# Two batches of a gated attention and expert kernel run as one program, with new engine orders in the batch loop

## What is computed

```python
x = x + tanh(g_xattn) * attention(layernorm(x), ctx, ctx)      # 16 heads of 16 channels
h = layernorm(x)
bids = sigmoid(h @ conf_w.T + conf_b) * wealth                 # [tokens, 8]
top_bids, selected = top_k(bids, 2)
combine = sum(one_hot(selected) * softmax(top_bids)[..., None])
x = x + tanh(g_ffn) * sum_e combine_e * expert_e(h)            # down(silu(gate h) * up h)
```

## Time and profile before

| | us |
|---|---|
| median of three runs | 1085.46 |
| lowest and highest | 1083.96, 1087.34 |
| the profiled execution | 1083.07 |
| its span, first to last instruction | 1081.4 |
| mean granted TensorE clock, share of full speed | 0.969 |

### The profile page before, as it was taken

How to read it: one execution, slowest core, us unless ns; L and a number is a source line. 1 busy time by engine, 2 the same in 40 slices (tenths; PEclk the granted TensorE clock), 3 DMA queues, 4 the chain that set the end, 5 groups by cost and what they waited for, 6 DMA issues and landing times.

```text
span 1081.4 us, 25127 instructions
## 1 busy us (share of the span) xinstructions
PE 1001.3 (93%) x8750; PEld 855.2 (79%) x8750; DVE 610.8 (56%) x1519; ACT 502.0 (46%) x796; POOL 366.3 (34%) x439
## 2 busy tenths in 40 slices
PE   5789999999999997759999999999999999999993
PEld 4556777777777765448999999999799999999993
DVE  3556777777777776455544444444554444444452
ACT  4366777777777774334323232332433323233321
POOL 1124555555555552443322212121332212122121
PEclk8799999999999999869999999999999999999997
DMA  8000111111111119258712111121262212121211
GB/s 254 27 22 22 43 45 47 41 41 41 43 51 58 41 39 371 77 182 323 256 25 40 25 35 35 25 37 23 42 229 49 37 23 40 20 40 23 37 35 17
DMA packets 48338, 77.30 MB, mean 71 GB/s; under 512 B 8616, under 2 KB 42152, under 8 KB 44456
## 3 DMA queue, kind: packets, MB, share of 16 engines
q0 software_dynamic: 18080, 50.15, 16.7%
q1 hardware_dynamic: 30216, 26.62, 8.3%
HBM read 52.09 MB, written 24.40 MB: 71 GB/s over the span
## 4 chain that ended last, share of the span: by engine, by line
PE 81%; ACT 5%; issue 4%; DVE 3%; POOL 3%; DMA 1%; SPq 1%; POOLq 1%; ACTq 0%; DVEq 0%
PE gate L1485 17%; PE up L1485 17%; PE down L1499 11%; PE down L1501 6%; PE pv L590 4%; PE scores L579 4%; PE misc L486 4%; PE scores L540 3%; PE maxps L554 2%; PE misc L513 2%; PE misc L522 2%; POOL K_rest L1204 2%; ACT probs L771 1%; PE misc L624 1%; PE turned L1468 1%
## 5 line engine op out<-in xcount | busy, mean ns | idle before, releaser
L1937 POOL DMA_INDIRECT out<-y,token x64 | 100.9, 1577 | 424.8 <-DVE y L1806 323.8
L1696 ACT ACTIVATE silu<-gate 128x512 f32<-128x512 f32 x128 | 76.8, 600 | 281.6 <-PE up L1485 281.6
L984 DVE TENSOR_REDUCE max_neg<-maxps 128x4 f32<-128x1024 f32 x128 | 156.5, 1222 | 60.2 <-PE maxps L554 60.2
L1485 PE MATMUL gate<-x_hi,w_split 128*128 128x256 f32 x1024 | 185.0, 282 | 2.0 <-DVE x_lo L1772 1.6
L1797 DVE TENSOR_TENSOR h<-silu,up 128x512 f32<-128x512 f32 x128 | 88.1, 688 | 174.8 <-ACT silu L1696 174.8
L1499 PE MATMUL down<-w_split,h_hi 128*128 128x512 f32 x512 | 185.9, 398 | 0.0
L1485 PE MATMUL up<-x_hi,w_split 128*128 128x256 f32 x1024 | 184.4, 282 | 0.0
L771 ACT ACTIVATE probs<-scores 128x1024 f32<-128x1024 f32 x124 | 127.2, 1026 | 80.5 <-PE scores L579 79.5
L1485 PEld LDWEIGHTS gate<-x_hi,w_split 128*128 128x128 f32 x1024 | 149.4, 189 | 5.5 <-issue 2.7
L1485 PEld LDWEIGHTS up<-x_hi,w_split 128*128 128x128 f32 x1024 | 148.8, 189 | 0.0
L1501 PE MATMUL down<-w_split,h_lo 128*128 128x256 f32 x512 | 144.1, 281 | 0.0
(11 more groups left out here) (204 smaller groups left out, 1586.3 us busy)
## 6 DMA issues: line engine op xcount, KB each, us to landing
stage<-gate_up_T POOLq DMA_DIRECT2D x20, 1024.0 KB, 8.1
stage<-down_T POOLq DMA_DIRECT2D x10, 1024.0 KB, 11.1
xg<-dispatched SPq DMA_DIRECT2D x34, 272.0 KB
ctxT<-ctxT SPq DMA_DIRECT2D x17, 256.0 KB, 2.8
x_all<-x SPq DMA_DIRECT2D x16, 256.0 KB, 5.2
out<-x_all SPq DMA_DIRECT2D x16, 256.0 KB, 2.2
dispatched<-pads SPq DMA_DIRECT2D x4, 272.0 KB, 3.6
dispatched<-pads POOLq DMA_DIRECT2D x4, 272.0 KB, 4.3
```

The source lines that it names most:

```text
L984: V.tensor_reduce(to, maxps[:], AX.X, ALU.max, negate=True).then_inc(s["max_taken"], 1)
L1485: last = mm(bank[:, i, :], into_inner(w, pair, mat)[:, c, cols], r[:, c, :], start=m == 0, stop=m == len(terms) - 1)
L1696: nc.scalar.activation(silu[pair % 2][:], gate[pair % 2][:], ACT.Silu).then_inc(s_silu, 1)
L1937: pool.indirect_dma_start(out, bass.IndirectOffsetOnAxis(token[:, t:t + 1], axis=0), y[:, t, :], None, compute_op=ALU.add).then_inc(s_adde ...
```

## The change

The change does these things:

- **Order of the loop, TensorE.** `project_q` is cut into halves: one stands between scores 5 and 6 with their maxima, one between maxima 6 and scores 7. Scores 5 come ahead of maxima 5. The turn of x2 moves behind stack K1, the turn of the maxima ahead of `weigh` 3, the logits between stacks Q0 and Q1. Stack Q0 is written to the banks of the maxima (`beside`) and so waits for no unit of `scores`.
- **Order of the loop, ScalarE.** The key read moves ahead of the read of oT and of exps 3. The reads of pv (head outputs) come sooner. `second_weight` moves from behind exps 4 to behind exps 5 and the read of pv 1. `norm_x2` moves behind exps 7; the sigmoid moves to the end, behind the reads of Q0 and Q1.
- **Order of the loop, VectorE.** `first_choice` moves behind `read_v`, `positions` ahead of the reduction of pair 5, `read_maxima` ahead of `read_logits`.
- **Ranks.** `macc` gets a second slice, made in `second_choice`, so that `ranks` is two matmuls for five; `positions` has 13 links for 14.
- **The two last batches** are one program, `last_two`, on every engine.

```diff
-        FULL = ["V", "TO0", "TO1", "K", "TN", "WO", "TX", "RK", "Q", "TX2", "LG", "MT"]
+        FULL = ["V", "TO0", "TO1", "K", "TN", "WO", "TX", "RK", "Q", "TX2", "MT", "LG"]
...
+        BESIDE = "Q0"
...
+        beside = maxps[:].rearrange("p u t s -> p (u t) s")
...
-                for t in range(QT):
-                    mm(use.bank("RK")[:, t, 0:EXPERTS], before[:], m12[:, t, :], start=True, stop=False)
-                    if t == 1:
-                        mm(use.bank("RK")[:, t, 0:EXPERTS], ones[:], m12[:, 0, :], start=False, stop=False)
-                    last = mm(use.bank("RK")[:, t, 0:EXPERTS], ones[:], macc[:], start=False, stop=True)
-                last.then_inc(s["misc_written"], 1)
+                mm(use.bank("RK")[:, :, 0:EXPERTS], before[:], m12[:], start=True, stop=False)
+                mm(use.bank("RK")[:, :, 0:EXPERTS], ones[:], macc[:], start=False, stop=True).then_inc(s["misc_written"], 1)
...
                 def stack_ahead(what):
-                    if ahead:
-                        stack(b + 2, what[0], int(what[1]), unit(b, what))
+                    if ahead and what == BESIDE:
+                        stack(b + 2, what[0], int(what[1]), None, beside)
+                    elif ahead:
+                        stack(b + 2, what[0], int(what[1]), unit(b, what) - (1 if UNITS[UNITS.index(what) - 1] == BESIDE else 0))
...
                 weigh(b, par, 1)
+                score(b, par, 5)
                 max_of_next(5)
-                score(b, par, 5)
                 if ahead:
-                    project_q(use)
+                    project_q_half(0, use)
                 score(b, par, 6)
+                max_of_next(6)
+                if ahead:
+                    project_q_half(1, use)
+                score(b, par, 7)
+                max_of_next(7)
+                weigh(b, par, 2)
+                stack_ahead("K1")
                 if back:
                     turn_x2(b - 1, 1 - par, use)
-                max_of_next(6)
-                score(b, par, 7)
-                weigh(b, par, 2)
-                max_of_next(7)
-                stack_ahead("K1")
+                if nxt:
+                    turn_maxima(b + 1, use)
+                weigh(b, par, 3)
+                stack_ahead("Q0")
                 if back:
                     logits(use)
-                if nxt:
-                    turn_maxima(b + 1, use)
-                stack_ahead("Q0")
-                weigh(b, par, 3)
                 stack_ahead("Q1")
...
                 exps(b, 2)
+                if ahead:
+                    read_k(b + 2, use)
                 if back:
                     read_whole(oT[:], "TN", use)
                 exps(b, 3)
+                read_pv(b, 0)
                 if ahead:
-                    read_k(b + 2, use)
                     norm_x(b + 2)
                 exps(b, 4)
+                stack_ahead("K0")
+                if ahead:
+                    read_whole(xT[:], "TX", use)
+                exps(b, 5)
+                read_pv(b, 1)
                 if late:
                     second_weight(b - 2)
-                read_pv(b, 0)
-                if ahead:
-                    read_whole(xT[:], "TX", use)
-                stack_ahead("K0")
-                exps(b, 5)
-                if back:
-                    norm_x2(b - 1, 1 - par)
-                read_pv(b, 1)
                 exps(b, 6)
                 if ahead:
                     read_q(b + 2, use)
                 exps(b, 7)
                 if back:
-                    read_whole(x2T[:], "TX2", use)
+                    norm_x2(b - 1, 1 - par)
                 read_pv(b, 2)
                 stack_ahead("K1")
                 if back:
-                    sigmoid(use)
+                    read_whole(x2T[:], "TX2", use)
+                read_pv(b, 3)
                 stack_ahead("Q0")
                 stack_ahead("Q1")
-                read_pv(b, 3)
+                if back:
+                    sigmoid(use)
...
-                V.tensor_tensor(m12[:], m1[:], m2[:], ALU.add).then_inc(s["masks_ready"], 1)
+                V.tensor_tensor(m12[:], m1[:], m2[:], ALU.add).then_inc(s["masks_made"], 1)
+                dve.wait_ge(s["masks_made"], b + 1)
+                if not is_first(b):
+                    dve.wait_ge(s["rows_ready"], b)
+                V.tensor_tensor(macc[:, 1, :], macc[:, 0, :].bitcast(fp32), m12[:, 0, :].bitcast(fp32), ALU.add).then_inc(s["masks_ready"], 1)
...
-                if late:
-                    first_choice(b - 2)
                 if ahead:
                     stats_x(b + 2)
                 if nxt:
                     read_v(1 - par, use)
+                if late:
+                    first_choice(b - 2)
                 max_of_next(0)
...
                 max_of_next(4)
-                max_of_next(5)
                 if late:
                     positions(b - 2, par, use)
+                max_of_next(5)
                 max_of_next(6)
                 max_of_next(7)
+                if nxt:
+                    read_maxima(b + 1, use)
                 if back:
                     read_logits(b - 1, use)
-                if nxt:
-                    read_maxima(b + 1, use)
```

## The result

The changed kernel takes **1200.63 us** (median; 1199.69 to 1202.85), the kernel before 1086.4 in the same runs: ratio 1.106, 95% interval 1.104 to 1.108. The direction was as forecast, the size was not: 50 us above the forecast of 1150 and 26 above the upper end of the range.

The account below looks back on a forecast made before the run. TensorE's order was taken to pace the loop, so its waits are paid twelve times: 1083.07 + 52.7 (waits and moved work) + 13 (clock) = 1148.8 us, or 1151.2 against the median, so 1150; range 1122 to 1175.

Parts of the forecast that it names:

- The sum: Whole kernel: 1083.07 + 52.7 for the loop + 13 for the clock = 1148.8 us, forecast as 1150.
- The clock: TensorE behind the maxima 6 wait: half clock adds 1.1 us an iteration, 13 in all; bounds nothing and 1.8 more.
- rival 2: Clock falls at both waits of an iteration, costing 1.8 us more each iteration: 1172 us; chance 0.15.
- first_choice behind read_v, +1.72: VectorE, ahead of the first reduction: eight links of about 0.2 us delay the second maxima product by 1.72 us.
- Key read and ranks: TensorE up to the key stack: no K_rest wait and fewer ranks products win back 0.60 of 1.72 us.
- has that much room: Reduction 3's product absorbs second_choice's new 0.2 us macc link once all is late; otherwise 2.4 us in all.
- Scores 5: TensorE, scores 5 ahead of maxima 5: waits some 0.3 us for the stack's bank; delay so far +1.42 us.
- positions: VectorE ahead of reduction 5: links wait for ScalarE's ed, so maxima 6 makes TensorE stand 2.97 us.
- rival 3: Only one VectorE delay bites, 2.6 or 2.7 us an iteration: 1117 us; chance 0.11.
- The rest, 8.33: From maxima 6 to the next iteration: 8.33 us instead of 6.76, making the iteration 4.39 us longer.
- The tail, 0 with bounds of -6.5 to +2: Last two batches as one program: gains offset by batch 12's scatter delaying batch 14's norm; net 0, -6.5 to +2.
- Rival 4 (faster): VectorE's new order hides in the loop, only won gaps count, 0.86 us an iteration: 1075 us; chance 0.07.

Follow-up runs that it names:

- e9: e3 with first choice behind reduction 3, residual behind reduction 4, GpSimd's context split and bias sum behind the query split, ahead of the scatters; 1108.1 us.
- e4: Changed kernel with redundant key-product matmuls ahead of maxima 1 and query-product matmuls ahead of maxima 6, filling the waits; 1175.8 us.
- e14: e11 with the first half of the query product run three extra times ahead of itself, filling the wait; 1129.2 us.
- e11: Kernel before with only positions moved ahead of reduction 5 and second_weight behind the read of pv 1; 1168.7 us.
- e5: Changed kernel with GpSimd's context split and bias sum moved ahead of the scatters in the loop; 1194.6 us.
- e7: e3 with GpSimd's context split and bias sum ahead of the query split and the scatters; 1116.1 us.
- e12: Kernel before with ScalarE's key read ahead of the oT read and exps 3, and ranks as two matmuls; 1087.1 us.
- e6: Changed kernel with batch 12's routing (second choice, ranks, positions, scatter) sooner in the tail, loop untouched; 1197.3 us.
- e13: Changed kernel with the loop bodies of before, leaving only last_two and the ranks as two matmuls; 1089.9 us.
- e10: e9 with the last two batches as two turns of before's loop body instead of one program; 1110.7 us.
- e1: Changed kernel with ScalarE's second_weight put back right behind exps 4; 1172.4 us.
- e3: Changed kernel with first choice behind reduction 2, second choice behind reduction 6, positions behind read_maxima, ranks and second_weight later; 1154.2 us.
- e2: Changed kernel with first_choice moved behind reduction 2, right ahead of second_choice; 1177.7 us.
- e8: e7 with the sooner tail routing of batch 12 from e6; 1115.1 us.

## Why the prediction was wrong, step by step

**The sum.** The loop's 110.5 us are 64.6 of idle, 44.3 of clock (337.7 less e9's 293.4) and 1.5 of work. The prediction had 65.7 for the loop: 52.7 of waits and moved work and 13 of clock. So some 31 us of the miss are the clock, some 13 the loop's waits and work, 11.6 the tail, less 2.1 in the prologue: together the 54 us by which the profiled execution (1202.85) missed 1148.8. Iterations took 32.6 to 35.7 us, where 29 to 31 were foreseen.

- **The clock: the step that failed.** I let it fall behind the long wait only and priced the half product, maxima 6 and scores 7: 1.1 us an iteration. It was 3.7, more than my upper bound of 2.9. The stretch from 324.6 to 331.0 holds 6.29 us of work at half clock, some 3.1 lost, because weigh 2 and stack K1 lie in it too; and in ten of the twelve iterations the clock fell at maxima 1 as well, as in rival 2, which had a chance of 0.15 and too small a price. e4 and e14 show that filling the idle time brings the clock back, e11 that one long wait an iteration is enough to lose 39 us. The Trainium skill ("TensorE: Matmul & The Clock Gate", section "HAM oscillation — how this bites in real kernels") says that a loop with a long wait in every turn drops the clock in every turn. e11 agrees: the clock falls in each of its iterations and is 0.87 over its loop.
- **first_choice behind read_v, +1.72: right mechanism, too small.** The chain took 2.5 us (304.64 to 307.16), since one link (L1109) took 0.92 instead of 0.2. It ends at 306.14, GpSimd's bias sum at 306.10. e5 took that sum away and the link was 0.18, maxima 1's wait 1.7. The Trainium skill ("SBUF — State Buffer", section "SBUF: two separate sides") has the rule: a VectorE operation with two SBUF inputs and a GpSimd operation that reads SBUF hold one pair of ports by turns, and the later one stands until the other has ended. Rows of e5, e7, e9 and e12 agree. I hadn't asked what runs on GpSimd at the place to which I saw the links go.
- **Key read and ranks: half right.** The wait for K_rest went. That the product behind the macc link of second_choice "has that much room" was wrong: K_rest, now earlier, runs beside that link, and maxima 4 waits 0.3 to 0.6 us in seven of the twelve iterations (316.55 above; alone in e12).
- **Scores 5: right**, 0.21 us for some 0.3.
- **positions: right.** Predicted 2.97 us at maxima 6 and a wait for ed; measured 2.8 to 3.2, and 1.8 for ed, twelve times. Of rival 3 (one delay alone, 2.7 an iteration) e11 shows how wrong its price was: 6.2.
- **The rest, 8.33:** 10.99 from maxima 6 to the next iteration here (324.71 to 335.70) and in two more iterations, 9.5 to 9.7 in the other nine. That is the half clock again.
- **The tail, 0 with bounds of -6.5 to +2:** +11.6. The place was named (batch 12's scatter ahead of batch 14's norm), but not priced: 7.77 us of wait. e6 took it away and got 3 us, not clear of noise. The new program costs 3 to 6 us on before's loop (e13); even before's tail is longer behind e9's loop (e10: 88.9, against 82.55 in before and 85.0 in e12, whose tail is before's but for the ranks). In the changed kernel the tail's growth is idle time (35.9 us against 25.2, window less busy), in e6, e10 and e13 it is mostly busy time at a lower clock (63.3 to 64.1 us at 0.72 to 0.74). Why the clock falls more there isn't settled, nor whether that busy time is what lengthens the tail.
- **Rival 4 (faster):** VectorE's new order didn't hide, for the reason given there: maxima 1 starts 1.28 us after its reduction (307.31 to 308.59), as in the rows before, and that reduction is late.

## What to carry to other kernels

In a loop that TensorE paces, price a new wait of some 3 us at up to twice its length: the idle time, and up to as much again in matmuls at half clock behind it (e11: 35.7 us of idle more than before, 39.2 of clock; the changed kernel 64.6 and 44.3; e1 53.7 and 22.7). Before a chain of short links is moved on VectorE, list what GpSimd does at the new place, and before one is moved later, who waits for its result on the other queues (e3). A saving in front of a wait is none (the ranks in e13), and where an order has no slack left, as here between a reduction and the next maxima, an operation that comes earlier can cost as much as it saves (e12).

## What the hardware showed that I had not expected

Waits of 1.0, 0.5 and 1.0 us an iteration (e4), or of 1.5 and 0.7 (e7), left the clock at 0.99 to 1.00; one of 1.7 and one of 2.9 (e5) left it at 0.86, no higher than 2.5 and 2.9 did. The length of a wait alone doesn't tell whether the clock falls behind it: behind 1.7 us (e5, maxima 1) it fell in eleven of twelve iterations, behind 2.3 us (e2, maxima 4) in five. In the changed kernel a link with one input, L1107 at 338.09, took 1.02 us, too, and ended with the bias sum beside it (337.80 for 1.28). And the prologue's end varied between kernels that are the same up to there, 93.9 us in e8 and 95.7 in e7, while before's iterations repeat to 0.02 us from the third on.
